# Cross-attention and feed-forward layer on one core: remaining keys as tiles of 32 rows, with new bank and order tables

## What is computed

```python
# x: (8, 256, 256), context: (8, 77, 256); 16 heads of 64; hidden size 768
xn = layernorm(layernorm(x)) * gamma + beta
q  = (xn @ w_q); k, v = split(context @ w_kv)          # 16 heads of 64
a  = softmax(q @ k.T / 8)                               # per head, 77 keys
x  = x + (concat(a @ v) @ w_out + b_out) * tanh(gate)
h  = layernorm(x)
x  = x + (silu(h @ wg.T) * (h @ wu.T)) @ wd.T           # weights are integers / 127
```

## Time and profile before

| | us |
|---|---|
| median of 3 runs (lowest, highest) | 296.05 (295.01, 296.74) |
| the profiled execution, its own time | 297.51 |
| span of the profiled execution | 295.7 |
| outside the span | 1.8 |

### The profile page before, as it was taken

How to read it: one execution, slowest core, us unless ns; L and a number is a source line. 1 busy time by engine, 2 the same in 40 slices (tenths; PEclk the granted TensorE clock), 3 DMA queues, 4 the chain that set the end, 5 groups by cost and what they waited for, 6 DMA issues and landing times.

```text
span 295.7 us, 6752 instructions
## 1 busy us (share of the span) xinstructions
PE 285.9 (97%) x2509; PEld 262.9 (89%) x2509; DVE 231.1 (78%) x609; ACT 158.8 (54%) x312; POOL 172.1 (58%) x198
## 2 busy tenths in 40 slices
PE   8999999979999999999999999999999999999895
PEld 7998978868988898989898989898999889988794
DVE  1598887777898789878987897788878878886853
ACT  4646875548268633853484358326842773354142
POOL 2653864358959681966396549635872778145033
PEclk9999999999999999999999999999999999999979
DMA  6995147332432113011201120112012101110001
GB/s 198 384 368 153 34 115 243 147 97 109 145 107 80 24 32 97 0 40 43 73 0 40 42 73 2 39 53 59 3 41 76 35 3 42 41 34 2 0 26 51
DMA packets 26668, 23.32 MB, mean 79 GB/s; under 512 B 12602, under 2 KB 24866, under 8 KB 26634
## 3 DMA queue, kind: packets, MB, share of 16 engines
q1 hardware_dynamic: 26634, 22.86, 24.9%
HBM read 15.87 MB, written 4.62 MB: 69 GB/s over the span
## 4 chain that ended last, share of the span: by engine, by line
PE 86%; DVE 6%; ACT 2%; issue 2%; SPq 1%; DMA 1%; POOL 1%; DVEq 0%
PE ps L904 13%; PE ps L849 10%; PE ps L808 6%; PE ps L816 5%; PE ps L812 5%; PE ps L973 5%; PE ps L977 5%; PE ps L974 5%; PE ps L738 5%; PE ps L831 4%; PE ps L957 3%; PE ps L960 3%; PE ps L925 2%; PE ps L771 1%; PE ps L746 1%
## 5 line engine op out<-in xcount | busy, mean ns | idle before, releaser
L1224 POOL TENSOR_TENSOR probs<-probs,total 128x512 f32<-128x512 f32 x32 | 33.6, 1049 | 59.6 <-DVE total L1363 59.5
L1250 POOL TENSOR_TENSOR h_lo<-hid,h_hi 128x256 fp32r<-128x256 f32 x42 | 30.9, 737 | 29.9 <-ACT h_hi L1137 29.5
L1239 POOL TENSOR_TENSOR t_lo<-t_all,t_hi 128x1232 fp32r<-128x1232 f32 x16 | 45.6, 2852 | 3.8 <-ACT t_hi L1095 3.8
L1067 ACT COPY pt<-ps 128x512 f32<-128x512 f32 x32 | 18.9, 591 | 40.8 <-PE ps L831 40.8
L973 PE MATMUL ps<-wo_hi,o_hi 128*128 128x256 f32 x128 | 36.3, 283 | 0.0
L974 PE MATMUL ps<-wo_lo,o_hi 128*128 128x256 f32 x128 | 36.1, 282 | 0.0
L977 PE MATMUL ps<-wo_hi,o_lo 128*128 128x256 f32 x128 | 36.0, 281 | 0.0
L1083 ACT CAST o_hi<-ps 128x512 fp32r<-128x512 f32 x32 | 17.2, 591 | 27.0 <-PE ps L849 27.0
L1346 DVE TENSOR_REDUCE top<-ps 128x4 f32<-128x308 f32 x64 | 28.7, 473 | 3.4 <-PE ps L816 3.1
L808 PE MATMUL ps<-t_hi,xn_hi 128*128 128x308 f32 x128 | 30.7, 321 | 0.0
L1371 DVE TENSOR_TENSOR o_lo<-ps,o_hi 128x512 fp32r<-128x512 f32 x32 | 20.6, 686 | 12.5 <-ACT o_hi L1083 12.2
(11 more groups left out here) (168 smaller groups left out, 838.2 us busy)
## 6 DMA issues: line engine op xcount, KB each, us to landing
x_ln<-in_x SPq DMA_DIRECT2D x8, 256.0 KB, 2.9
v_scratch<-v_out SPq DMA_DIRECT2D x4, 512.0 KB, 3.3
v_whole<-v_scratch SPq DMA_DIRECT2D x16, 128.0 KB
stream<-in_x SPq DMA_DIRECT2D x8, 256.0 KB, 2.9
x_rooms<-in_x SPq DMA_DIRECT2D x7, 256.0 KB, 7.7
out<-stream SPq DMA_DIRECT2D x7, 256.0 KB, 2.2
wk_raw<-in_L_xattn_w_kv SPq DMA_DIRECT2D x4, 256.0 KB, 5.2
wq_raw<-in_L_xattn_w_q SPq DMA_DIRECT2D x1, 1024.0 KB, 7.9
```

Of the source, the lines that this page charges most:

```text
L1224: nc.gpsimd.tensor_tensor(whole, whole, scale.to_broadcast([P, HR, HALVES, KEYS_WHOLE]), ALU.mult).then_inc(probs_done, 1)
L1239: nc.gpsimd.tensor_tensor(t_lo[:, :, cols], t_all[:, :, n, cols], t_hi[:, :, cols].bitcast(F32), ALU.subtract).then_inc(tlo_done, 1)
L1250: nc.gpsimd.tensor_tensor(h_lo[:, f, :], hid_of(b, f), h_hi[:, f, :].bitcast(F32), ALU.subtract).then_inc(hlo_done, 1)
```

## The change

Five things change together.

1. The remaining keys of a pair of heads (j, 0) and (j, 1) lie in one tile of 32 partitions, 26 of them used. A value stage has eight `v_whole` products as before and eight `v_rest` products on 26 rows by 64 columns, four row tiles by two column halves. Each j has its own bank: three fixed ones (3, 4, 5) and one from the shared rotation, which V0 and V1 now enter. For these, scores give up bank 2.
2. The "t" jobs rotate over bank pairs in another way, and ACT and DVE share their copies in another way.
3. In the opening SP loads w_out in four DMAs and not eight, and spreads the `v_rest` loads of batch 0: six of eight before the fourth value store and not two.
4. Round 0 has orders of its own for PE and DVE (`PE_FIRST`, `DVE_FIRST`). In all other rounds DVE does Z2 before LN, and ACT does t0 between the two halves of X.
5. In the end, POOL and not DVE normalises the first tile (`la`), DVE takes R1.7 earlier among the small steps, PE does two dummy products (`wu`) before g0, and the last down product is in three pieces (d, m, e) and not two.

```diff
-MISC_BANKS = (6, 7, 3)
-SCORE_BANKS = (0, 1, 2)
-LAST_BANKS = (4, 5, 7, 6, 0, 1)
-LAST_X1T_BANKS = (0, 2)
-LAST_DOWN_BANKS = (2, 3)
+MISC_BANKS = (6, 7, 2)
+SCORE_BANKS = (0, 1)
+VALUE_BANKS = (3, 4, 5)
+LAST_BANKS = (4, 5, 2, 6, 0, 1)
+LAST_X1T_BANKS = (0, 3)
+LAST_DOWN_BANKS = (3, 7)
+FORMER_GATE_BANK = 6
...
-DVE_ORDER = "LN1 M2 LN Z2 X1 M3 O0 H0 Z3 H1 H2 M0 H3 H4 O1 Z0 H5 M1 R0 Z1 R1 AG Y0 Y1".split()
-ACT_ORDER = "Ta C0 C1 E2 X1 O0 X WO t0 t1 E3 t2 h0 C2 Tb t3 h1 C3 h2 t4 E0 h3 O1 h4 t5 h5 E1".split()
+DVE_ORDER = "LN1 M2 Z2 LN X1 M3 O0 H0 Z3 H1 H2 M0 H3 H4 O1 Z0 H5 M1 R0 Z1 R1 AG Y0 Y1".split()
+ACT_ORDER = "Ta C0 C1 E2 X1 O0 X t0 XH WO t1 E3 t2 h0 C2 Tb t3 h1 C3 h2 t4 E0 h3 O1 h4 t5 h5 E1".split()
...
+PE_FIRST = "T0 S2 T1 X1T S3 V0 XT G0 G1 T2 G2 G3 S0 T3 G4 G5 V1 S1 D0 O0 O1 D1".split()
+DVE_FIRST = "M2 LN Z2 X1 M3 O0 H0 Z3 H1 H2 H3 M0 H4 O1 Z0 H5 M1 Y0 R0 Z1 R1 AG".split()
...
-PE_END = "O0.7 O1.7 G5.7 p0 p1 xa xb g0 q0 q1 g1 g2 g3 g4 g5 d0 d1 e0 e1".split()
+PE_END = "O0.7 O1.7 G5.7 p0 p1 xa xb wu g0 q0 q1 g1 g2 g3 g4 g5 d0 d1 m0 m1 e0 e1".split()
...
-DVE_END = ("Z3.7 H0.7 H1.7 H2.7 H3.7 H4.7 O1.7 R0.7 na0 na1 na2 na3 na4 na5 na6 na7 na8 na9 na10 na11 R1.7 nb0 nb1 la nb2 nb3 "
+DVE_END = ("Z3.7 H0.7 H1.7 H2.7 H3.7 H4.7 O1.7 R0.7 na0 na1 na2 na3 na4 na5 na6 na7 na8 R1.7 nb0 na9 nb1 na10 nb2 na11 nb3 "
...
-POOL_END = "P3.7 h0.7 h1.7 B.7 h2.7 h3.7 h4.7 h5.7 h0.8 h1.8 h2.8 h3.8 h4.8 h5.8".split()
+POOL_END = "P3.7 h0.7 h1.7 B.7 h2.7 h3.7 h4.7 la h5.7 h0.8 h1.8 h2.8 h3.8 h4.8 h5.8".split()
...
-ACT_TS = "1 3 5 6 8 10 12 13 15".split()
+ACT_TS = "0 1 3 5 7 8 10 12 14".split()
+T_BANKS_FIRST = (0, 2, 6)
+T_BANKS = (4, 2, 6, 0)
...
-        shared = [n for n in PE_ORDER if n in ("X1T", "XT", "G0", "G1", "G2", "G3", "G4", "G5", "D0", "D1", "O0", "O1")]
+        shared = [n for n in PE_ORDER if n in ("X1T", "XT", "V0", "V1", "G0", "G1", "G2", "G3", "G4", "G5", "D0", "D1", "O0", "O1")]
...
+                if n[0] == "V":
+                    return olo_done, NU * b + 2 * k + 1
...
+            def keep_warm():
+                for _ in range(2):
+                    mm(ps[:, LAST_BANKS[0], 0:P], ident[:], ident[:], start=True, stop=True)
...
-                for pair in range(2):
-                    for keys in (v_whole, v_rest):
-                        for e in range(2):
-                            j = 2 * pair + e
-                            at = j if keys is v_whole else HR
-                            for r in range(HALVES):
-                                half = slice(r * KEYS_WHOLE, r * KEYS_WHOLE + (KEYS_WHOLE if keys is v_whole else HR * NEW))
-                                ins = mm(ps_p[e * DH:(e + 1) * DH, r, pair * Q:(pair + 1) * Q],
-                                         keys[half, g, j * DH:(j + 1) * DH], pt[half, at, :],
-                                         start=keys is v_whole, stop=keys is v_rest)
+                claim(b, f"V{g}")
+                for turn in range(2):
+                    for r in range(HALVES):
+                        for j in range(HR):
+                            if (j // 2 + j + r) % 2 == turn:
+                                e = (r + j) % 2
+                                half = slice(r * KEYS_WHOLE, (r + 1) * KEYS_WHOLE)
+                                mm(ps[e * DH:(e + 1) * DH, value_bank(g, j), 0:Q],
+                                   v_whole[half, g, j * DH:(j + 1) * DH], pt[half, j, :], start=True, stop=False)
+                for e in range(2):
+                    for j in range(HR):
+                        part = slice(j * REST, j * REST + HALVES * NEW)
+                        ins = mm(ps[e * DH:(e + 1) * DH, value_bank(g, j), 0:Q],
+                                 v_rest[part, g, e * DH:(e + 1) * DH], pt[part, HR, :], start=False, stop=True)
```

More of the change, by code:

```diff
@@ L348, in banks_of @@
             if j[0] == "t":
-                at = 2 * ((n - first_t) % 4)
+                m = n - first_t
+                at = T_BANKS_FIRST[m] if m < len(T_BANKS_FIRST) else T_BANKS[m % len(T_BANKS)]
                 return [at, at + 1]
@@ L366, in xattn_ffn_kernel @@
         act_jobs += [copied_at[s] for s in ACT_FILLS]
-        dve_jobs += [copied_at[s] for s in DVE_ORDER if s in copied_at and s not in ACT_FILLS]
+        dve_jobs += [copied_at[s] for s in DVE_FIRST if s in copied_at]
         by_act = {n: i + 1 for i, n in enumerate(act_jobs)}
@@ L406, in gate_up_psum, with value_bank, value_psum, value_chunks @@
         def gate_up_psum(b, f):
-            return ps[:, LAST_BANKS[f], :] if last(b) else ps[:, bank[f"G{f}"], :]
+            if last(b):
+                return ps[:, LAST_BANKS[f], :]
+            return ps[:, FORMER_GATE_BANK if b == B - 1 and f == FC - 1 else bank[f"G{f}"], :]
+        def value_bank(g, j):
+            return bank[f"V{g}"] if j == 0 else VALUE_BANKS[j - 1]
+        def value_psum(g, i):
+            at = bank[f"V{g}"] if i == 0 else VALUE_BANKS[0]
+            return ps[:, at:at + (1 if i == 0 else HR - 1), 0:Q]
+        def value_chunks(g, i):
+            return slice(HR * g, HR * g + 1) if i == 0 else slice(HR * g + 1, HR * (g + 1))
         def tile(t):
@@ L587, in load_v_rest @@
                 for j in heads:
-                    first = r * KEYS_WHOLE + j * NEW
-                    sp.dma_start(v_rest[first:first + NEW, :, j * DH:(j + 1) * DH], by_head[rest_keys[r], r, j]).then_inc(v_in, 16)
+                    first, e = j * REST + r * NEW, (r + j) % 2
+                    sp.dma_start(v_rest[first:first + NEW, :, e * DH:(e + 1) * DH], by_head[rest_keys[r], r, j]).then_inc(v_in, 16)
             def load_v(n):
@@ L628, in _ @@
             sp.wait_ge(s_job, last_t + 1)
-            out_rows = w_out.rearrange("(g n e r d) m -> e g r d n m", g=2, e=2, r=HALVES, d=DH)
+            out_rows = w_out.rearrange("(i j r d) m -> j r d i m", j=2, r=HALVES, d=DH)
+            wo_pairs = wo_raw.rearrange("p (i j) m -> p j i m", j=2)
             def load_wo(*which):
-                for i in which:
+                for j in which:
                     for e in range(2):
-                        sp.dma_start(wo_raw[e * DH:(e + 1) * DH, 2 * i:2 * i + 2, :],
-                                     out_rows[e, i // HALVES, i % HALVES]).then_inc(s_in["wo"], 16)
+                        sp.dma_start(wo_pairs[e * DH:(e + 1) * DH, j], out_rows[j, (e + j) % 2]).then_inc(s_in["wo"], 16)
             load_ln(1)
-            load_wo(0, 1, 2)
+            load_wo(0)
             for r in range(RC):
@@ L995, in stages_of @@
                     stages[f"q{t}"] = ("start", down_piece, B - 1, t, FC - 1, FC, general)
-                    stages[f"d{t}"] = ("start", down_piece, B, t, 0, FC - 1, general)
+                    stages[f"d{t}"] = ("start", down_piece, B, t, 0, FC - 2, general)
+                    stages[f"m{t}"] = ("start", down_piece, B, t, FC - 2, FC - 1, general)
                     stages[f"e{t}"] = ("start", down_piece, B, t, FC - 1, FC, general)
@@ L1000, in stages_of @@
                 stages["FL"] = ("start", transpose_largest)
+                stages["wu"] = ("start", keep_warm)
                 return stages
@@ L1137, in split_h @@
                 nc.scalar.copy(h_hi[:, f, :], hid_of(b, f)).then_inc(hhi_done, 1)
-            stages = {"X1": ("ffn", split_x2), "X": ("next", affine_x),
+            stages = {"X1": ("ffn", split_x2), "X": ("next", affine_x), "XH": ("next", split_x),
                       "Ta": ("next", split_t, 0), "Tb": ("next", split_t, 1)}
@@ L1265, in _ @@
                 stages[f"h{f}"] = ("ffn", split_h, f)
+            stages["la"] = ("start", normalise_x1_first_tile)
             stages["XS"], stages["XS2"] = ("start", x_scales, 0, FIRST_X), ("first", x_scales, FIRST_X, B)
@@ L1510, in _ @@
                 name = "ab"[t]
-                stages["l" + name] = ("start", normalise_x1_tile, t)
                 stages["x" + name] = ("start", split_x2_tile, t)
@@ L1514, in _ @@
                     stages[f"n{name}{i}"] = ("start", scale_step_tile, t, i)
+            stages["lb"] = ("start", normalise_last_tile)
             for b in range(FIRST_X, B):
@@ L1523, in _ @@
             start(DVE_START, stages)
-            first_round(DVE_ORDER, stages)
+            first_round(DVE_FIRST, stages)
             other_rounds(DVE_ORDER, stages, DVE_END)
```

88 lines of the change are left out of this document (51 added, 37 removed).

## The result

The changed kernel takes 302.36 us, median of 4 runs (302.17 to 302.82), and the kernel before 295.94 (295.01 to 296.74, 4 runs): a ratio of 1.0208, with a 95% interval of 1.0175 to 1.0241. It is 2.1% slower, where the forecast was 293.5 us and faster, and 302.4 lies outside the range of 288 to 298.

A forecast was written before the change was run, and what follows sets the result against it. PE, 97% busy, was taken as the bound. Opening and round 0 -2.3, rounds 1 to 6 +1.2, last round +1.0, end -2.45 sum to -2.55 us: 294.96 from 297.51, so 293.5 for the median; range 288.0 to 298.0.

The forecast's parts named there:

- Part 1: Value stages: eight v_rest tiles side by side save 0.435 us, the shape change costs 0.15; 0.28 us saved each.
- (a): Steady rounds: with two score banks, S3 waits for the first subtraction of S2, some 0.23 us late.
- (b): Steady rounds: G1 takes V0's bank, waits for its first low part behind LN, and stalls some 0.55 us.
- (c): Steady rounds: V1 takes G3's bank, waits for H3, starts 0.47 us later; net +0.2 us a round.
- (d): Last round: V1.7 waits for H3.7 and O0.7 for H4.7; +1.0 us, savings included.
- Parts 2 and 3: Opening and round 0: T-bank waits go, gaining 0.7 and 0.5 us; the v_rest load wait goes, gaining 0.95.
- Part 4: Round 0: V0 and V1 save 0.56 us, D0 before O0 costs 0.44, T2 fills a hole, counted as nothing.
- Part 5: The end: earlier x1 tile, covered h_lo wait and a clock that stays up; -2.45 us, without the clock -0.85.
- The last step of the sum: Whole kernel: 294.96 us for the profiled execution, which lay 1.46 above the median, so 293.5 for the median.
- slower by the waits: Rival, rounds: DVE, ACT and POOL's chain costs 0.9 us a round, not 0.2; +4.2 us, 297.7; chance 0.10.

The follow-up runs named there:

- e11: The changed kernel with LN before Z2 on DVE and h1 before B on POOL, every v_rest product made twice: 299.59 us, ratio 1.0116.
- e5: The changed kernel with LN back in front of Z2 on DVE and h1 in front of B on POOL: 292.80 us, 0.9879 of before.
- e10: From e5, h1 before t3 on ACT in the last round, and round 0 ended as in the kernel before: 292.34 us, 0.9877.
- e2: The kernel before with only Z2 put in front of LN in DVE's order of a steady round: 297.08 us, ratio 1.002.
- e3: The changed kernel without the two dummy products (wu) at the end: 302.42 us, ratio 1.0185.
- e8: The kernel before with h1 in front of B on POOL: 295.83 us, ratio 0.9998.

## Why the prediction was wrong, point by point

- **Part 1, the value product: right.** Forecast -0.28 us a stage with eight tiles side by side; V0 to XT took 1.90 us before and 1.64 now (115.83 to 117.47), -0.26. e11 puts eight v_rest records at 0.20 us. The change of shape, taken at 0.15, is near 0.1: V0's first v_rest record starts 1.02 us after V0 (115.83 to 116.85), where four groups of 0.22 and the entry's 0.05 make 0.93.
- **(a), two score banks: right**, S3 0.2 us late (0.57 us behind the start of the x1 transposes, from 113.35 to 113.92; before 114.17 to 114.52, 0.35). The loss is still in e5's 28.06.
- **(b), the step that failed.** "Now its 0.67 us (0.73 less overlap) come after Z2": place and mechanism were right, and the wait of G1 for V0's bank too (forecast 0.55, measured 0.59), but LN behind Z2 doesn't take 0.73 us. It runs into POOL's P2, which starts as soon as Z2's reciprocal is there, and takes 1.43. The duration was carried over from a place where POOL was idle. Of the 0.7 us more, X1 passes some on to G0 (+0.28) as well, which the prediction took as on time. By the table the place of LN costs 0.9 to 1.1 us a round; the forecast has 0.55 for it.
- **(c), V1 and H3: right in kind, wrong in size.** It was taken that V1 would be no later for H3 than it is for G1 anyway. By the table V1's claim costs 0.35 us of its own in the changed kernel and 0.55 with LN in front. "+0.2 a round" was +1.05, and "+1.2" for the rounds +6.3. That is 5.1 us of a miss of 8.9: with e5's two orders, which remove both waits, a round is 0.47 us shorter than before.
- **(d), the last round: right.** +1.0 forecast, +0.92 measured; PE waits 1.17 us at V1.7.
- **Parts 2 and 3: right.** V0 of round 0 starts at 60.13, from 62.41: 2.28 earlier, where the three terms give 2.15. The three waits are gone.
- **Part 4: too low.** D0 in front of O0 was charged 0.44 and measured 0.47 (e10), as forecast; but V0 to V0 of round 0 grew by 0.66 us in all, and the forecast had it shrink by 0.12. Of PE's waits in that stretch, the one for x_hat (0.7 us, before 0.3) is down to 0.2 in e10, so it belongs to D0. Two new ones of 0.5 us each stay in e10: T2, "ahead of G2", waits for V0's low part, where the forecast had it fill a hole, and the last scores ahead of round 1 wait for their bank. What each costs by itself wasn't tried. The opening as a whole gave 1.63 and not 2.3 us.
- **Part 5: nearly right up to PE's last product.** Forecast -2.45, of which 1.6 for the clock and 0.85 for the rest. From O0.7 to PE's last product it is -2.00 (23.26 to 21.26). e2, with the old end at full clock, needs 21.83, so the clock is 1.43 of it and the rest 0.57. The dummies have no part in it (e3). The span shows only 1.01, since the stretch behind PE's last product is 0.99 us longer, which the forecast had at nothing.
- **The last step of the sum: wrong.** The forecast takes 1.6 us for the clock off the profiled execution, and then another 1.46 because this execution "lay 1.46 above the median". But that excess is the clock's fall itself, in the main: executions of the kernel before with that clock lie 1.3 us above those without (297.1 and 295.9, at e3). So the clock was counted twice. Against a median whose execution doesn't lose the clock, only 0.95 us of the forecast's 2.55 are left, 295.1 us. This is 1.5 us of the miss; the rounds are 5.1, the stretch behind PE's last product 1.0, the opening with round 0 0.7, and part 5 0.45.
- **The rivals.** What came is the one called "slower by the waits", at 0.9 a round and a chance of 0.10; it named M0 and the copies as what slips, and it was LN, and H3 behind POOL's B. Its time, 297.7 us, is still 4.7 short: it shares the step with the clock, and the rounds lost 1.05.

## What to carry to other kernels

A duration read from a trace holds beside the neighbours that it had there. Before an instruction is moved, look up what the other engines do at its new place; a DVE instruction that reads and writes SBUF, as LN does, may be held for the rest of a POOL instruction. When a profiled execution lies above the median, ask what it holds that the median doesn't before a saving is taken off both. When a buffer gets a new holder, follow the chain that frees it through every engine's order and re-order that chain with it: the same change was 2.1% slower with the old POOL order and a misplaced LN, and 1.2% faster with two swaps. And test the order edit in both kernels: e2 and e8 show that neither swap changes the time by more than can be told without the new banks.

## What the runs showed of the hardware that was not expected

- DVE's tensor_scalar from SBUF to SBUF (128x256, 0.41 us alone) is blocked by a running POOL instruction, to 1.14 us beside one of 1.12 and to 2.34 us beside one of 2.80, and ends 0.15 us after it in both. DVE's instructions that read the scores from PSUM weren't held: in the changed kernel a pair of subtractions takes 0.85 us both at 113.40, with POOL idle, and at 118.71, beside t_lo.
- Eight records on tiles of 32 rows and 64 columns run side by side in 0.20 us (e11), about the time of a group of four on 64 rows (0.22).
- The granted clock fell to 0.50 for 3.4 us behind 3.00 us in which PE was busy for 1.72 (the kernel before and e8), and stayed at 1.00 in e2 behind a stretch with 1.73. The fall differs between executions of the same end, and costs 1.4 us there.
